# Big-head attention with scores as three float32r products of two-term splits

## The chip, the cores and the metric

The program runs on one core of a Trainium2 chip. The metric is the device time of one launch in microseconds, lower is better. The kernel before was timed three times: 2041.05, 2045.54 and 2047.98 us, median 2045.54 us. The profile shown here is one further execution, whose span from the first to the last instruction is 2040.1 us.

## The reference, cut to what matters

The reference is a two-layer transformer over 2048 tokens of width 128. Each layer is an attention followed by a mixture of experts. The change is in the attention of the second layer that has eight heads of 128:

```
qkv = einsum('bnc,fc->bnf', xn, w_qkv)            # xn: 2048 x 128, normalised
q, k, v = ...                                     # 8 heads of 128
sim  = einsum('bihd,bjhd->bhij', q * 128**-0.5, k)
sim  = where(j > i, -max, sim)                    # causal
attn = softmax(sim)
out  = einsum('bhij,bjhd->bihd', attn, v)  ->  x @ w_out
```

Everything is float32, and the scores and products are computed in float32 (the small-head attention elsewhere in the kernel uses bfloat16 terms).

## The kernel before, in words

The stage is `big_head_attention`, from about 874 to 1449 us of the span. Weights are folded beforehand: for each head, `A[:, h, :]` is the product of the query and key weights and `B` the product of the value and output weights. So a score tile is x (keys) times G, where G = A of the head times x (queries), and head outputs are added straight into `X`.

Work is cut into 32 *atoms*: a block of 512 queries and a head, (qb, h). Blocks 1 and 0 come first, alternating for each head, so the even atoms 0 to 14 are qb 1 and the odd atoms 1 to 15 are qb 0; then eight atoms of qb 2 (16 to 23), and eight of qb 3 (24 to 31). An atom has 4(qb+1) tiles of 128 keys, of which the last four lie on the diagonal and are 512, 384, 256 and 128 queries wide. Its life is:

1. `query(a)`: TensorE forms G in PSUM bank 5 (`G_BANK`, L2086), ScalarE copies it to `GT` (L2146).
2. `score(a, kt)`: TensorE forms one tile in one of five banks (L2103), ScalarE copies it to `ST` (L2158), GpSimd masks a diagonal tile (L2044), VectorE folds it into a running maximum `M` (L2204, L2207).
3. `reduce`: GpSimd takes the maximum over the partitions (L2052). Then the event `subtract`: VectorE subtracts it from all tiles of the atom (groups of four tiles L2215, the four diagonal ones L2219), and ScalarE takes the exponential (L2165, L2169).
4. `product(a, kt, half)`: TensorE multiplies by the values (L2122), in two halves of the atom; after each half VectorE divides and adds to `X` (`accumulate`, L2228 and L2232).

During the first atoms TensorE also forms the values (L2093). `ST` holds eight groups of four tiles, so for qb 2 and 3 only two atoms are under way at once: scores of atom a+1 come before the products of atom a.

The order of all this is one list, `plan.events`, laid by `KeyPlan`. Every engine walks the same list in order and takes its own part of each event, with semaphores between the engines. `KeyPlan` runs a clock of its own: each event advances it by an assumed cost. A score tile costs 0.02 + columns/600 us, a query 0.86, a product 0.265 for each 128 columns. Some events go in when that clock passes a due time: `reduce` of an atom right after the first event that follows its scores, and `subtract` 4.5 us after that, at the first event that is *not* a score (line `while self.spreads and event[0] != "score" and ...` of `emit`). Where a block normalisation for the next stage is due (events `measure`, `normalize`, `fold` behind atom 27) it is placed by that clock too.

A `query(a+1)` stands at the head of the scores of atom a, so G is formed a whole atom ahead; `GT` has three buffers, and the scores of atom a+1 are the first to need its copy.

Elsewhere, in the opening of the first stage, a table `place` of 0 and 1 is made for the small-head attention: VectorE clears it (L2374) and GpSimd fills it with 24 small copies from the identity (L2371), before it starts on its share of the first rotation.

Of the kernel before, what the change touches and what calls it, by code (L numbers as in the profile page):

```python
# [15 lines left out]
F32 = mybir.dt.float32  # L16
BF16 = mybir.dt.bfloat16
# [233 lines left out]
def small_head_stage(core, tag, src_T, w, bias, cs, arrived, KS, QS, V, place, kbias, OT, causal, order, beyond,  # L251
# [20 lines left out]
    with ExitStack() as st:  # L272
# [86 lines left out]
        with nc.Block() as block:  # L359
# [160 lines left out]
            def _(pe):  # L520
# [27 lines left out]
                def place_set(s, v):  # L548
# [9 lines left out]
                    for t in range(TERMS):  # L558
                        for i, u in enumerate(SETS[v]):
                            rows = slice(32 * i, 32 * (i + 1))  # L560
                            mm = pe.matmul(ps[:, 4 + i, :], place[rows, which, t, u, :],
# [1298 lines left out]
class KeyPlan:  # L1860
# [8 lines left out]
    def __init__(self):  # L1869
# [14 lines left out]
        self.wide0 = [sum(n - 1 for n in self.groups[:a]) for a in range(len(self.atoms) + 1)]  # L1884
        self.events = []
        self.clock, self.turns, self.spreads, self.norms = 0.0, [], [], []
        self.asked = 0
        self.lay()

# [9 lines left out]
    def emit(self, event, us):  # L1899
# [6 lines left out]
        while self.norms and self.clock >= self.norms[0][0]:  # L1906
            self.events.append(self.norms.pop(0)[1])

    def turn(self):
        _, a = self.turns.pop(0)  # L1910
        self.events.append(("reduce", a))
        if a == NORM_ATOM:
            behind = max(n for n, (qb, h) in enumerate(self.atoms) if qb in EARLY_BLOCKS)
            for n, g in enumerate(EARLY_BLOCKS):
                self.norms += [(self.clock + 0.5 + n, ("measure", g, behind)), (self.clock + 12.0 + 2 * n, ("normalize", g)),
                               (self.clock + 17.0 + 3 * n, ("fold", g))]
# [7 lines left out]
    def score(self, a):  # L1924
        if a + 1 < len(self.atoms):
            self.emit(("query", a + 1), 0.86)
        for kt in range(self.tiles[a]):
            self.emit(("score", a, kt), 0.02 + (BLK - self.first_col(a, kt)) / 600.0)
        self.turns.append((self.clock, a))

    def lay(self):
        NA = len(self.atoms)
        values = [(t, c) for t in range(NT) for c in range(2)]
        sent = 0
        self.emit(("query", 0), 0.86)
        for a in range(NA):
# [50 lines left out]
def big_head_attention(core, tag, xnT, X, raw, hpad, gamma, beta):  # L1987
# [15 lines left out]
    with ExitStack() as st:  # L2003
# [5 lines left out]
        GT = sb("GT", [P, 3, BLK])  # L2009
        M, row = sb("M", [P, 2, BLK]), sb("row", [P, 2, BLK])  # L2010
        rec = sb("rec", [P, 2, TPB])
        call = sb("call", [P, 3, 8])
# [6 lines left out]
        g_ready, g_done, s_ready, copied, masked = (sem(n) for n in ("g_ready", "g_done", "s_ready", "copied", "masked"))  # L2019
# [11 lines left out]
        with nc.Block() as block:  # L2031
# [37 lines left out]
            def _(pe):  # L2069
                asked, folded = [0], [0]  # L2070

                def fold(g):
                    pe.wait_ge(g_done, asked[0])
# [5 lines left out]
                def query(a):  # L2079
                    qb, h = plan.atoms[a]  # L2080
                    if a:
                        pe.wait_ge(g_done, a)
                    if folded[0]:
# [3 lines left out]
                              start=True, stop=True).then_inc(g_ready, 1)  # L2087

# [8 lines left out]
                def score(a, kt):  # L2097
                    n, c = plan.tile0[a] + kt, plan.first_col(a, kt)
                    if kt == 0:
                        pe.wait_ge(g_done, a + 1)  # L2100
# [27 lines left out]
                for event in plan.events:  # L2128
                    if event[0] == "query":
                        query(event[1])  # L2130
                    elif event[0] == "value":
# [9 lines left out]
            def _(act):  # L2141
                def query(a):
                    act.wait_ge(g_ready, a + 1)
# [424 lines left out]
```

## Time and profile before

| | |
|---|---|
| runs | 2041.05, 2045.54, 2047.98 us |
| span of the profiled execution | 2040.1 us |
| TensorE matmul busy | 1822.2 us (89%) |
| VectorE busy | 1547.6 us (76%) |
| ScalarE busy | 1380.9 us (68%) |
| GpSimd busy | 415.4 us (20%) |

The profiler took one execution; the program's time around that span is not in the trace. A matmul's busy time is from its start to a modelled end, so back-to-back matmuls overlap and a group of n of them lasts less than n times the mean of one: the pace of a stream is read from where a group starts and how many stand in it. "Idle before" is the time for which an engine had nothing to do before an instruction, with the instruction that ended it. A float32 matmul of the program is two MATMUL instructions in the trace, each with a weight load of its own.

### The profile page before, as it was taken

To read this page: it belongs to the slowest core of one execution; us is meant where nothing else is said; L and a number is where in the kernel's file an instruction comes from. 1 tells how busy PE (TensorE), PEld (TensorE's weight loads), DVE (VectorE), ACT (ScalarE), POOL (GpSimd) and SP (SyncE) were. 2 spreads that over 40 slices of the span, in tenths; PEclk is the share of its full clock that TensorE was granted. 3 is DMA by queue.
4 is the path that set the end of the run, shared out by engine and by line. 5 is a ranking of instruction groups with operands and counts; after the bars stand their busy time and mean duration, and the time that the engine had idled before them with its cause. 6 is when DMAs were issued, how large, how long until landed. Compare 5 with 4: busy or idle time off the path is not lost. (4 is left out here: it accounts for less than half of the span.)

```text
span 2040.1 us, 39849 instructions
## 1 busy us (share of the span) xinstructions
PE 1822.2 (89%) x15560; PEld 907.5 (44%) x15560; DVE 1547.6 (76%) x2263; ACT 1380.9 (68%) x2565; POOL 415.4 (20%) x650
## 2 busy tenths in 40 slices
PE   6699999999999798489989999999778999999784
PEld 2122222222223388435667776767512322233384
DVE  5899999999997443446767777877578979886434
ACT  3499999999999643255645656566347898888331
POOL 4201000000002324323432121221330101123413
PEclk8699999999999998889999999999867999999598
DMA  5000000000000378400000000000100000000274
GB/s 168 1 3 3 5 10 4 5 9 5 8 7 7 107 264 284 124 0 1 1 1 1 1 1 1 1 1 1 53 1 2 5 3 12 5 12 6 60 262 154
DMA packets 52874, 81.51 MB, mean 40 GB/s; under 512 B 9200, under 2 KB 37744, under 8 KB 52560
## 3 DMA queue, kind: packets, MB, share of 16 engines
q1 hardware_dynamic: 47520, 70.50, 10.9%
q0 software_dynamic: 3072, 6.30, 1.0%
q8 instruction: 124, 2.03, 0.4%
q10 hardware_dynamic: 2096, 2.17, 0.4%
q14 instruction: 62, 0.51, 0.1%
HBM read 64.13 MB, written 12.06 MB: 37 GB/s over the span
## 5 line engine op out<-in xcount | busy, mean ns | idle before, releaser
L826 DVE TENSOR_REDUCE a_mx<-psum 128x2 f32<-128x1024 f32 (+2 forms) x832 | 906.1, 1156 | 73.2 <-PE psum L601 40.2
L752 ACT ACTIVATE a_cs<-psum 128x512 f32<-128x512 f32 (+3 forms) x1664 | 857.0, 572 | 80.7 <-PE psum L619 62.4
L642 PE MATMUL psum<-a_cs,a_V 128*16 128x256 f32 (+1 forms) x6400 | 501.7, 384 | 20.9 <-ACT a_OD L732 9.7
L601 PE MATMUL psum<-a_KS,a_QS 48*128 48x512 bf16 (+3 forms) x1664 | 324.9, 381 | 32.9 <-DVE a_mx L826 29.7
L619 PE MATMUL psum<-a_QS,a_KS 51*128 51x512 bf16 (+3 forms) x1664 | 336.6, 378 | 4.9 <-ACT a_cs L752 3.1
L2122 PE MATMUL psum<-b_VW,b_ST 128*128 128x129 f32 x2176 | 252.5, 277 | 13.3 <-DVE X L2232 13.3
L2122 PEld LDWEIGHTS psum<-b_VW,b_ST 128*128 128x128 f32 x2176 | 248.5, 194 | 15.0 <-DVE X L2232 15.0
L619 PEld LDWEIGHTS psum<-a_QS,a_KS 51*128 51x128 bf16 x1664 | 87.7, 93 | 355.0 <-ACT a_cs L752 310.3
L2103 PE MATMUL psum<-b_GT,AT 128*128 128x512 f32 (+3 forms) x640 | 242.9, 534 | 1.6 <-ACT b_ST L2158 1.6
L642 PEld LDWEIGHTS psum<-a_cs,a_V 128*16 128x16 f32 x6400 | 107.1, 94 | 244.7 <-issue 120.2
L2207 DVE TENSOR_TENSOR b_M<-b_M,b_ST 128x512 f32<-128x512 f32 (+3 forms) x288 | 174.8, 607 | 43.1 <-ACT b_ST L2158 12.6
L2165 ACT ACTIVATE b_ST<-b_ST 128x2048 f32<-128x2048 f32 x48 | 91.7, 1911 | 137.5 <-DVE b_ST L2215 137.5
L2158 ACT ACTIVATE b_ST<-psum 128x512 f32<-128x512 f32 (+1 forms) x320 | 157.5, 535 | 38.2 <-PE psum L2103 37.0
L2103 PEld LDWEIGHTS psum<-b_GT,AT 128*128 128x128 f32 x640 | 122.6, 192 | 135.1 <-issue 116.1
L470 POOL CAST a_mterm<-a_mxr 128x16 bf16<-128x16 f32 x32 | 6.8, 212 | 703.1 <-DVE a_mxr L831 703.1
L2044 POOL TENSOR_SCALAR_AFFINE_SELECT b_ST<-b_ST 128x128 f32<-128x128 f32 x128 | 68.0, 555 | 368.8 <-ACT b_ST L2158 367.9
L601 PEld LDWEIGHTS psum<-a_KS,a_QS 48*128 48x128 bf16 x1664 | 83.6, 94 | 124.0 <-DVE a_mx L826 105.3
L1711 DVE TENSOR_TENSOR e_prod<-e_gate,psum 128x384 f32<-128x384 f32 (+1 forms) x72 | 43.3, 602 | 105.1 <-ACT e_gate L1669 104.5
L1613 PE MATMUL psum<-e_xT,e_W 128*128 128x128 f32 x876 | 113.5, 282 | 9.3 <-issue 7.9
L2215 DVE TENSOR_TENSOR b_ST<-b_ST,b_row 128x2048 f32<-128x2048 f32 x48 | 107.7, 2286 | 13.3 <-POOL b_row L2052 13.3
L1613 PEld LDWEIGHTS psum<-e_xT,e_W 128*128 128x128 f32 x876 | 107.6, 199 | 11.0 <-issue 7.7
L1669 ACT ACTIVATE e_gate<-psum 128x384 f32<-128x384 f32 (+1 forms) x72 | 38.0, 528 | 86.3 <-PE psum L1613 79.6
(225 smaller groups left out, 1514.5 us busy)
## 6 DMA issues: line engine op xcount, KB each, us to landing
e_W<-in_l_experts SPq DMA_DIRECT2D x45, 576.0 KB, 5.5
e_W<-in_l_experts SPq DMA_DIRECT2D x21, 768.0 KB, 5.8
yg<-e_yout SPq DMA_DIRECT2D x14, 256.0 KB, 6.0
xg<-zeros SPq DMA_DIRECT2D x2, 1472.0 KB, 9.8
a_cs<-in_rope ACTq DMA_DIRECT2D x4, 512.0 KB, 9.5
a_QS<-a_mrow SPq DMA_DIRECT2D x128, 3.0 KB
a_cs<-in_rope SPq DMA_DIRECT2D x1, 2048.0 KB, 7.8
a_num<-a_OD SPq DMA_DIRECT2D x120, 16.0 KB
```

Source lines behind the costliest of these rows:

```text
L601: mm = pe.matmul(ps[:, 2 * slot + half, 0:width], QS[rows, 2 * p + i, q_cols(qb, qt * P, P)], KS[rows, 2 * p + i, c * BLK:c * BLK + width] ...
L619: pe.matmul(ps[:, plan.bank(entry), c:BLK], KS[rows, 2 * p + i, kt * P:(kt + 1) * P], QS[rows, 2 * p + i, q_cols(qb, c, BLK - c)], start=T ...
L642: mm = pe.matmul(ps[32 * j:32 * j + 2 * HD, AV_BANK, a:b], V[:, kt, HPP * p + j, :], probs(e, a, b), start=(kt == 0 and half == 0), stop=last,
L752: act.activation(probs(HPP * s + j, c, BLK), ps[:, plan.bank(entry), c:BLK], ACT.Exp, scale=scale).then_inc(exp_done, 1)
L826: dve.tensor_reduce(mx[:, pk % 2, qt, 2 * i:2 * i + 2, c], banks, AX.X, ALU.max).then_inc(max_done, 1)
L1613: mm = pe.matmul(ps[:, 2 * side + n % 2, c * P:(c + 1) * P], weight(j, a, a + P), xT[:, j % 2, :], start=True, stop=True)
L2103: pe.matmul(ps[:, n % S_BANKS, c:BLK], xnT[:, kt * P:(kt + 1) * P], GT[:, a % 3, c:BLK], start=True, stop=True).then_inc(s_ready, 1)
L2122: mm = pe.matmul(ps[:, O_BANK + half, cols], ST[:, plan.at[a][kt // TPB], kt % TPB, i * P:(i + 1) * P], VW[:, kt, h, :], start=(kt == 0 an ...
L2158: act.activation(tile(a, kt), ps[:, n % S_BANKS, c:BLK], ACT.Copy).then_inc(copied, 1)
L2165: act.activation(group, group, ACT.Exp, scale=scale).then_inc(wide_exp, 1)
L2207: dve.tensor_tensor(M[:, a % 2, c:], M[:, a % 2, c:], tile(a, kt), ALU.max).then_inc(max_done, 1)
L2215: dve.tensor_tensor(group, group, row[:, a % 2, :].unsqueeze(1).broadcast_to([P, TPB, BLK]), ALU.subtract).then_inc(wide_sub, 1)
```

## The change

The scores of the big heads are no longer float32 products. The keys `xnT` are split once into a high part `XH` (rounded to float32r by a ScalarE copy) and a low part `XL` (VectorE, the difference); this is the new event `part`, for one block of 512 keys each. G is split too: ScalarE copies it rounded to `GH`, TensorE adds minus the identity times `GH` to the same PSUM bank (`remainder`), and ScalarE copies what is left there to `GL`. A score tile is then the sum of three float32r matmuls, XL·GH + XH·GL + XH·GH, in one bank. `GH` and `GL` have two buffers each where `GT` had three.

```
+                def remainder(a):                                  # TensorE
+                    pe.wait_ge(split, plan.copy["query", a])
+                    ...
+                    pe.matmul(ps[:, G_BANK, :], minus[:, :], GH[:, a % 2, :], start=False, stop=True,
+                              skip_group_check=True).then_inc(g_ready, 1)
                 def score(a, kt):
-                    pe.matmul(ps[:, n % S_BANKS, c:BLK], xnT[:, kt * P:(kt + 1) * P], GT[:, a % 3, c:BLK],
-                              start=True, stop=True).then_inc(s_ready, 1)
+                    pe.matmul(out, XL[:, keys], GH[:, a % 2, c:BLK], start=True, stop=False)
+                    pe.matmul(out, XH[:, keys], GL[:, a % 2, c:BLK], start=False, stop=False)
+                    pe.matmul(out, XH[:, keys], GH[:, a % 2, c:BLK], start=False, stop=True).then_inc(s_ready, 1)
...
+                def part(g):                                       # ScalarE
+                    act.activation(XH[:, mine], xnT[:, mine], ACT.Copy).then_inc(split, 1)
                 def query(a):                                      # ScalarE
-                    act.activation(GT[:, a % 3, :], ps[:, G_BANK, :], ACT.Copy).then_inc(g_done, 1)
+                    act.activation(GH[:, a % 2, :], ps[:, G_BANK, :], ACT.Copy).then_inc(split, 1)
+                def remainder(a):                                  # ScalarE
+                    act.wait_ge(g_ready, 2 * a + 2)
+                    act.activation(GL[:, a % 2, :], ps[:, G_BANK, :], ACT.Copy).then_inc(split, 1)
...
+                dve.tensor_scalar(minus[:, :], core.ident[:, :], -1.0, None, ALU.mult).then_inc(low, 1)
+                def part(g):                                       # VectorE
+                    dve.wait_ge(split, plan.copy["part", g])
+                    dve.tensor_tensor(XL[:, mine], xnT[:, mine], XH[:, mine].bitcast(F32), ALU.subtract).then_inc(low, 1)
```

The list of events changes with it. `part` 0 and 1 stand at its head, part 2 before the scores of atom 14 and part 3 before those of atom 22. `remainder(a+1)` stands after the third score tile of atom a. The planner's cost of a score tile is 0.02 + columns/800, and the block normalisations are placed a little differently:

```
     def score(self, a):
+        if a in self.parts:
+            self.emit(("part", self.parts[a]), 0.0)
         if a + 1 < len(self.atoms):
             self.emit(("query", a + 1), 0.86)
         for kt in range(self.tiles[a]):
-            self.emit(("score", a, kt), 0.02 + (BLK - self.first_col(a, kt)) / 600.0)
+            self.emit(("score", a, kt), 0.02 + (BLK - self.first_col(a, kt)) / 800.0)
+            if kt == 2 and a + 1 < len(self.atoms):
+                self.emit(("remainder", a + 1), 0.22)
...
-                self.norms += [..., (self.clock + 12.0 + 2 * n, ("normalize", g)), (self.clock + 17.0 + 3 * n, ("fold", g))]
+                self.norms += [..., (self.clock + 12.0 + 4 * n, ("normalize", g)), (self.clock + 16.0 + 4 * n, ("fold", g))]
```

So that the new tiles fit, `place` is cut from eight planes to two (128x3072 words to 128x768). GpSimd first adds the four column groups of the identity together (three additions of 128x32), and the 24 copies then move 16 elements for each partition instead of 64:

```
+        span = len(SETS) * 2 * HD
+        groups = [self.core.ident[:, i * span:(i + 1) * span] for i in range(P // span)]
+        pool.tensor_tensor(mine, groups[0], groups[1], ALU.add).then_inc(self.made, 1)
+        for i in range(2, len(groups)):
+            pool.wait_ge(self.made, i - 1)
+            pool.tensor_tensor(mine, mine, groups[i], ALU.add).then_inc(self.made, 1)
...
-                    pool.tensor_copy(rows, heads[:, :, j, :]).then_inc(self.made, 1)
+                    pool.tensor_copy(rows, self.heads[:, :, j, :]).then_inc(self.made, 1)
```

## Rows read from the trace of the kernel before

**Rows 1.** Busy time by stretch: us, each engine's busy (instructions), granted clock, DMA.

```profile
945.00:1050.00 105.00, 97.84 (x565) 73.31 (x565) 84.06 (x179) 59.71 (x120) 44.01 (x52) 1.00 0.00 1
1105.00:1205.00 100.00, 100.00 (x562) 72.59 (x562) 74.45 (x123) 57.82 (x95) 21.16 (x25) 1.00 0.00 1
```

**Rows 2.** Timeline, TensorE: start, us, what, count; 20 us, then one atom of qb 2.

```profile
20.20 0.83 PE L561 MATMUL psum<-a_terms,place 32*128 32x512 bf16 x12 [1.70 <-POOL a_terms L444]
...
1136.75 7.09 PE L2122 MATMUL psum<-b_VW,b_ST 128*128 128x129 f32 x62
...
1143.67 1.02 PE L2086 MATMUL psum<-AT,big_raw 128*128 128x512 f32 x2
...
1144.53 9.19 PE L2103 MATMUL psum<-b_GT,AT 128*128 128x512 f32 x24
```

**Rows 3.** Groups by line and shape: busy and mean, idle before.

```profile
L2103 PE MATMUL psum<-b_GT,AT 128*128 128x512 f32 x448 | 201.4, 600 | 1.6 <-ACT b_ST L2158 1.6
```

**Rows 4.** Timeline, 1137 to 1157 us (atoms 19 and 20, qb 2): VectorE, ScalarE, GpSimd.

```profile
1139.47 4.49 DVE L2215 TENSOR_TENSOR b_ST<-b_ST,b_row 128x2048 f32<-128x2048 f32 x2
...
1145.81 1.53 ACT L2169 ACTIVATE b_ST<-b_ST 128x512 f32<-128x512 f32 x4
1147.24 0.57 ACT L2146 ACTIVATE b_GT<-psum 128x512 f32<-128x512 f32 x1
...
1148.87 7.85 DVE L2207 TENSOR_TENSOR b_M<-b_M,b_ST 128x512 f32<-128x512 f32 x11
...
1156.82 1.78 POOL L2052 PARTITION_ALL_REDUCE b_row<-b_M  x1 [0.87 <-DVE b_M L2207]
```

**Rows 5.** Timeline, 1011 to 1051 us (atoms 11 and 12, qb 0 and 1; last row atom 14's end).

```profile
1015.35 1.78 POOL L2052 PARTITION_ALL_REDUCE b_row<-b_M  x1 [0.87 <-DVE b_M L2207]
...
1017.52 4.67 DVE L2207 TENSOR_TENSOR b_M<-b_M,b_ST 128x512 f32<-128x512 f32 x7
...
1022.11 2.53 DVE L2219 TENSOR_TENSOR b_ST<-b_ST,b_row 128x512 f32<-128x512 f32 x4
1022.29 2.15 POOL L2052 PARTITION_ALL_REDUCE b_row<-b_M  x1 [0.87 <-DVE b_M L2207]
...
1025.28 2.28 DVE L2215 TENSOR_TENSOR b_ST<-b_ST,b_row 128x2048 f32<-128x2048 f32 x1
...
1030.85 0.57 ACT L2146 ACTIVATE b_GT<-psum 128x512 f32<-128x512 f32 x1
...
1050.13 0.57 ACT L2146 ACTIVATE b_GT<-psum 128x512 f32<-128x512 f32 x1
```

**Rows 6.** Timeline, atoms of qb 3: one round at 1249 us, the normalisations, the last atoms.

```profile
1249.19 0.57 ACT L2146 ACTIVATE b_GT<-psum 128x512 f32<-128x512 f32 x1
...
1250.82 11.04 DVE L2207 TENSOR_TENSOR b_M<-b_M,b_ST 128x512 f32<-128x512 f32 x15
...
1318.73 6.70 DVE L2215 TENSOR_TENSOR b_ST<-b_ST,b_row 128x2048 f32<-128x2048 f32 x3
...
1409.99 1.17 ACT L2158 ACTIVATE b_ST<-psum 128x512 f32<-128x512 f32 x2
...
1434.71 13.22 PE L2122 MATMUL psum<-b_VW,b_ST 128*128 128x129 f32 x116 [0.49 <-DVE X L2232]
```

**Rows 7.** Timeline, TensorE: matmuls that follow an idle time in brackets.

```profile
930.41 1.13 PE L2093 MATMUL psum<-big_raw,AT 128*128 128x512 f32 x2 [1.99 <-ACT b_VW L2150]
...
1054.60 8.62 PE L2122 MATMUL psum<-b_VW,b_ST 128*128 128x129 f32 x52 [3.54 <-DVE X L2232]
...
1076.12 6.07 PE L2122 MATMUL psum<-b_VW,b_ST 128*128 128x129 f32 x52 [0.78 <-DVE X L2232]
```

**Rows 8.** Busy time by stretch, as in rows 1: around those idle times.

```profile
1053.00:1060.00 7.00, 5.40 (x25) 5.40 (x26) 4.01 (x14) 1.55 (x4) 1.83 (x2) 0.51 0.00 0
...
928.00:931.00 3.00, 1.01 (x3) 0.30 (x2) 1.01 (x2) 2.36 (x7) 1.31 (x4) 1.00 0.00 0
```

**Rows 9.** Timeline, GpSimd in the opening.

```profile
8.19 4.32 POOL L2371 CAST place<-ident 128x64 bf16<-128x64 f32 x24 [7.69 <-DMA ident<-in_ident]
```

More of the change, by code:

```diff
@@ L16 @@
 F32 = mybir.dt.float32
+F32R = mybir.dt.float32r
 BF16 = mybir.dt.bfloat16
@@ L1884, in __init__ @@
         self.wide0 = [sum(n - 1 for n in self.groups[:a]) for a in range(len(self.atoms) + 1)]
+        self.reach = {g: min(a for a, n in enumerate(self.groups) if n > g) for g in range(NB)}
+        self.parts = {self.reach[g] - 2: g for g in range(2, NB)}
         self.events = []
         self.clock, self.turns, self.spreads, self.norms = 0.0, [], [], []
-        self.asked = 0
+        self.asked, self.whole = 0, False
         self.lay()
+        copies = [event[0:2] for event in self.events if event[0] in ("part", "query", "remainder")]
+        self.copy = {event: n + 1 for n, event in enumerate(copies)}
+        self.part = {event[1]: n + 2 for n, event in enumerate(event for event in copies if event[0] == "part")}
     def first_col(self, a, kt):
@@ L1905, in emit @@
             self.spread()
-        while self.norms and self.clock >= self.norms[0][0]:
+        if event[0] in ("query", "remainder"):
+            self.whole = event[0] == "query"
+        while self.norms and self.clock >= self.norms[0][0] and not (self.whole and self.norms[0][1][0] == "fold"):
             self.events.append(self.norms.pop(0)[1])
@@ L1934, in lay @@
         sent = 0
+        for g in range(2):
+            self.emit(("part", g), 0.0)
         self.emit(("query", 0), 0.86)
+        self.emit(("remainder", 0), 0.22)
         for a in range(NA):
@@ L2072, in fold @@
                 def fold(g):
-                    pe.wait_ge(g_done, asked[0])
+                    pe.wait_ge(split, plan.copy["remainder", asked[0] - 1])
                     if folded[0]:
@@ L2081, in query @@
                     if a:
-                        pe.wait_ge(g_done, a)
+                        pe.wait_ge(split, plan.copy["remainder", a - 1])
                     if folded[0]:
@@ L2130, in _ @@
                         query(event[1])
+                    elif event[0] == "remainder":
+                        remainder(event[1])
                     elif event[0] == "value":
@@ L2171, in _ @@
                 for event in plan.events:
-                    if event[0] == "query":
+                    if event[0] == "part":
+                        part(event[1])
+                    elif event[0] == "query":
                         query(event[1])
+                    elif event[0] == "remainder":
+                        remainder(event[1])
                     elif event[0] == "value":
```

46 lines of the change are left out of this document (30 added, 16 removed).

## The prediction

> **What bounds the kernel now.** I read the page's shares first, then the busy time by stretch over the stage, then the timeline of one atom in each of its three regimes, and last what TensorE's clock did after idle times.
>
> The first view invites a simple answer: TensorE is 93% busy where atoms of qb 1 and 0 alternate and 100% where qb 2 runs; the others stay near 80% or below [rows 1]. A cheaper score would then come off the time whole. The timelines say otherwise, so the reader should look there for a second loop.
>
> An atom of qb 2 has 12 score tiles in 24 instructions, worth 10.5 full tiles by their columns; less the last one's drain of 0.2 they take 9.0 of their 9.19 us [rows 2], so a full tile is 0.858 us, 0.429 an instruction. There are 448 such instructions, 224 full tiles [rows 3]. A query is the same 0.86 us. Products run at 0.112 us an instruction: 62 in 7.09 with the last one's 0.26 us drain [rows 2]. So TensorE needs for an atom of qb 2: 0.86 + 9 x 0.858 + 1.31 (diagonal tiles of 384, 256 and 128 columns in proportion) + 84 x 0.112 = 19.3 us.
>
> The other loop does not contain TensorE. ScalarE copies the tiles of atom a, VectorE folds them into the maximum, GpSimd reduces, VectorE subtracts, ScalarE exponentiates, and only then, in ScalarE's order, come G's copy and the tiles of atom a+1. In atom 20 [rows 4]: G's copy starts at 1147.24, folds end at 1148.87 + 7.85 = 1156.72, the reduction ends at 1158.60. The subtraction and exponentials then take what they took one atom earlier: subtraction starts at 1139.47, exponentials end at 1147.34, when the next G copy may start. That is 11.36 + 7.87 = 19.23 us. The folds in it stand at 0.795 us a full tile (11 in 7.85, the last three narrower: 0.795 is the step of the full ones in the timeline), though one tile comes every 0.858 from TensorE: five banks were filled ahead. Hence they are VectorE's own pace, and no faster score shortens them. TensorE and this loop are within 0.1 us of each other in qb 2.
>
> In qb 3 the loop is 24.5 us: G's copy 1249.19, folds end at 1250.82 + 11.04 = 1261.86, reduction 1.9, three subtractions 6.7 and the diagonal ones 1.6, tail 1.7 [rows 6, 4]. TensorE needs 0.86 + 13 x 0.858 + 1.31 + 116 x 0.112 = 26.3. There it is the bound, with 1.8 us to give for each atom. In the pairs of qb 1 and 0 the copies of G behind an even atom's exponentials stand 19.28 us apart (1030.85 and 1050.13 [rows 5]), while TensorE's work for a pair is 2 x 0.86 + 6 x 0.858 + 2 x 1.31 + 72 x 0.112 = 17.5. VectorE's chain sets that: the even atom's folds end at 1017.52 + 4.67 = 1022.19, subtraction of the odd atom 2.53, and GpSimd's reduction of the even atom (1022.29 to 1024.44) is hidden beneath it, so the even atom's subtraction starts at 1025.28.
>
> **The change part by part.**
>
> *Score tile on TensorE.* No float32r instruction is in the trace. Bounds: a float32 instruction of the trace takes 0.429 for 512 columns, so three such would be 1.29 us a tile (dearer than 0.858 by half). A one-pass product is bf16: 12 instructions over four row groups, three rounds, in 0.83 us with a drain of 0.38 leave 0.22 us a round [rows 2], so three are 0.65. I take 0.65, the row that moves one pass: a split into terms of fewer bits is what one pass can hold. For narrow tiles I take the same rate down to a floor of 0.11 an instruction, the shortest pace with its own weight load in rows 2: 0.49, 0.33, 0.33 against 0.65, 0.43, 0.22. In all TensorE gives back 224 x 0.21 + 32 x 0.15 = 52 us, less 32 remainders at 0.22 = 7: 45 us. The page "TensorE: Matmul & The Clock Gate" of the Trainium skill (LDWEIGHTS) gives a weight load as columns over 1.2, 107 ns for 128; the trace's 0.112 agrees. Without that floor the 128-wide tile would be 0.17, and the five rounds below would each be 0.15 us shorter.
>
> *qb 2, from atom 19 on.* The loop of 19.23 stays. GL's copy (0.57) lies between third and fourth tile, where ScalarE copies every 0.48 and VectorE takes 0.795: hidden. TensorE now needs 17.4 and waits about 1.8 us at each remainder, behind G's copy. Saving: 0.
>
> *Atom 14's end to atom 19.* Here TensorE was late. Before: from 1050.13 [rows 5] to G's copy of atom 19's round at 1147.24 - 19.25 = 1128.0, 77.9 us. After: products of atoms 11 and 12 end at +11.4, query and first tile +12.9, folds of atom 16 +13.7 to +22.1, subtraction +24.1 to +30.2, exponentials +32.0, then two loops of 19.2: +70.4. Saving 7.5.
>
> *qb 3.* Seven rounds from 1224.3 to the last at 1409.5 took 185.2. After: 7 x 24.5, plus 3.4 for the three variances that fill the time before 1318.73 [rows 6] beyond the reduction, plus 5.0 for ScalarE's stores and scalings in atom 28: 179.9. Saving 5.3. From 1409.99 the last atom ran to 1447.9, 37.9 us; now its scores end at +7.3, products of atom 30 at +20.2, its own (13.0) at +33, less 0.4: saving 5.2.
>
> *Pairs of qb 1 and 0: the order.* Reading `emit` with the new list: `subtract` of an odd atom is due 4.5 us after its scores on the planner's clock, at the first event that is no score. Before, that was the first product behind the even atom's eight tiles. Now a `remainder` stands after the third tile, at 2.65 + 0.86 + 2.0 + 0.2 = 5.7 on that clock, and `subtract` goes in there: atoms 5, 7, 9, 11, 13, five rounds. ScalarE's copies of tiles 4 to 8 are thereby queued behind the odd atom's exponentials, VectorE's folds behind its subtraction, and the even atom's reduction loses its cover. With G's copy at 0: odd folds end 3.7, three even folds 5.7 to 7.9, subtraction to 9.6 (1.7 with GpSimd idle), exponentials 10.3, fourth copy 10.8, folds 10.85 to 14.05 (masks included), reduction 15.9, subtraction 19.9, exponentials 21.6. Against 19.28: +2.3 a round.
>
> *Pairs: the clock.* In such a round TensorE also stops at the remainder until G's copy, and was done 5 to 6 us before. After 3.54 us idle, the products at 1054.60 took 8.62 for 52, against 6.07 after 0.78 idle [rows 7]; the granted clock from 1053 to 1060 was 0.51, that is 1.2 instead of 2.4 GHz. After 1.99 us idle it stayed 1.00 [rows 7, 8]. With some 4.5 us at the low level, 2.2 us of work come late; the path remainder, tile, products of the odd atom, query, first even tile (4.2 us) feeds the even folds: they start at 7.9 instead of 5.7. +2.1 more, 4.4 in all. The first round has an idle time of 2.4, so I take 3.0 for it: 3.0 + 4 x 4.4 = 20.6 lost. Bounds: 5 x 2.3 = 11.5 without clock falls, 5 x 5.6 = 28 with low stretches of the 6 us seen at 1054.60. The same page of the skill says that "the default state is throttled, and activity releases the throttle"; these rows agree.
>
> *Parts.* 0 and 1 run while TensorE forms the first G. Part 2 and 3 put a copy of 0.6 us in ScalarE's loop (as the 0.57 copy of rows 4): 1.1 lost. The values' stretch (874 to 940) gains 1.5, half a microsecond for each of its three even atoms, whose folds TensorE fed one by one. *Opening.* 24 copies in 4.32 us [rows 9] are 0.18 each for 64 elements; a quarter of that plus three additions gives 3.8, so 0.5 earlier; bounds -1.2 and +0.6. The clearing of `place` is before them and nothing waits for its length.
>
> *Sum.* 20.6 + 1.1 - 7.5 - 5.3 - 5.2 - 1.5 - 0.5 = +1.7 on the 2040.1 of the profile, which is its span; the runs' median lies 5.4 higher, so 2047 us.
>
> **The rivals.**
>
> *Full gain.* TensorE stays the bound and gives back its 45 us: 2000. For it: 100% busy [rows 1]. Against: 19.23 us loops without it, at the folds' own pace. Half-way, with VectorE faster than I hold, 2025.
>
> *The order costs, the clock doesn't fall:* 11.5 in place of 20.6, so 2038. For it: 1.99 us idle left the clock alone; against: 3.54 did not, and 5 to 6 are coming.
>
> *Slower: the rounds stretch further.* One mechanism: low clock at each resumption delays the even atom's first tile, hence its folds, hence the next G copy, so idle times lengthen to 7 us. It decides from 5 us of low clock: 28 to 33 lost in the five rounds, 2055 to 2060.
>
> *Float32r isn't one pass.* At 0.429 a product (upper bound above) TensorE's gain turns into 224 x 0.43 + 20 + 14 = +130, and hardly any of it is hidden: about 2165.
>
> **How the numbers follow.** Below 0.3%, 6 us, a measurement of this kernel can't be told from no change. Chances: forecast 0.42 (2041 to 2054), no clock fall 0.20 (2034 to 2041), full or half gain 0.12, stretched rounds 0.18, not one pass 0.08. Faster by over 6 us: 0.12 and most of the second, 0.28. Slower by over 6: 0.18 + 0.08 and the upper edge of the forecast, 0.35. Within: 0.37. Range 2030 to 2064: it leaves out the not-one-pass case and the full gain. The likeliest case's own is 2041 to 2054.
>
> **What would show it.** Right: float32r instructions 0.21 to 0.22 us apart; copies of G in the even rounds of atoms 6 to 14 some 23 to 24 us apart, with 5 us of TensorE idle before each remainder and granted clock 0.5 behind it; exactly 19.2 in qb 2 with TensorE under 95% busy; 24.5 in qb 3; folds still 0.795 apart. Wrong: copies of G less than 19 apart in qb 2, which would mean that VectorE's folds follow TensorE; rounds of 19.3 in the pairs, which would mean that the order costs nothing.

## The result and the profile after

The changed kernel took 2062.05 us (median of 4 runs, 2060.96 to 2062.59); the kernel before took 2046.76 us over the 4 runs that stand beside it (2041.05 to 2051.25). The ratio is 1.0077, 95% interval 1.0058 to 1.0096: slower by 15.3 us. The range of 2030 to 2064 holds it, by 2 us at its upper edge. The predicted 2047 is 15 us too low, and the likeliest case's own 2041 to 2054 misses it by 8. One execution was slow, of the last experiment: it took 2729.96 us at a granted clock of 0.57 and is left out of the median there.

The profiled execution spans 2060.8 us against 2040.1, and its granted clock is 0.92 against 0.94. I measure "the stage" as the time from the first query matmul on the big heads to the end of the last product: 573.4 us before, 588.5 after, +15.1. All the rest of the span was 1466.6 before and 1472.3 after, but over the profiles of six variants that leave it alone it lies anywhere from 1462.2 to 1475.5. So the stage is enough to explain the medians, and nothing finer can be read from the rest.

In the changed kernel L2104 is the query, L2181 the copy of G's high part, L2111 the remainder, L2185 the copy of G's low part, L2131 to L2133 the three score products, L2197 the tile copies, L2257 the folds, L2265 and L2269 the subtraction, L2151 the products with the values, L2278 and L2282 their accumulate. First the groups by line and shape, which answer to [rows 3] (busy us, mean ns of one, idle before):

```profile
L2131 PE MATMUL psum<-b_GH,b_XL 128*128 128x512 f32 x224 | 103.0, 460 | 0.0
L2132 PE MATMUL psum<-b_GL,b_XH 128*128 128x512 f32 x224 | 89.4, 399 | 0.0
L2133 PE MATMUL psum<-b_GH,b_XH 128*128 128x512 f32 x224 | 89.3, 399 | 0.0
L2111 PE MATMUL psum<-b_GH,b_minus 128*128 128x512 f32 x32 | 16.9, 527 | 46.7 <-ACT b_GH L2181 46.7
```

The mean of one includes its drain; the starts in the timeline are 0.227 to 0.228 us apart at full clock. A full tile thus costs 0.684 us where two float32 instructions cost 0.858: the scores did become cheaper. The last row is where TensorE now stops: 46.7 us of waits at the remainders for the copy of G, where the scores before waited 1.6 in all [rows 3]. 25 of them stand before the six remainders from 955 to 1075, in the pairs.

The stretches (columns as in [rows 1]; the pairs end later now, so the first is longer):

```profile
945.00:1070.00 125.00, 104.25 (x632) 93.17 (x630) 78.17 (x174) 59.76 (x127) 37.77 (x54) 0.88 0.00 1
1001.00:1008.00 7.00, 5.05 (x24) 4.96 (x25) 2.82 (x9) 3.69 (x10) 3.25 (x5) 0.53 0.00 0
...
1110.00:1210.00 100.00, 93.24 (x637) 83.35 (x637) 76.01 (x128) 60.15 (x102) 22.16 (x25) 1.00 0.00 1
```

In the pairs the granted clock is 0.88 on average, with stretches at half speed; before it was 1.00. In qb 2 TensorE fell from 100% to 93%, and no time came of it.

One pair's round in the timeline (start, us, engine, line, what, count, idle before and its releaser), which answers to [rows 5]:

```profile
1026.16 0.57 ACT L2181 ACTIVATE b_GH<-psum 128x512 fp32r<-128x512 f32 x1
...
1026.78 0.80 PE L2111 MATMUL psum<-b_GH,b_minus 128*128 128x512 f32 x1 [4.55 <-ACT b_GH L2181]
...
1027.91 4.17 PE L2151 MATMUL psum<-b_VW,b_ST 128*128 128x129 f32 x20
...
1031.92 1.02 PE L2104 MATMUL psum<-AT,big_raw 128*128 128x512 f32 x2
...
1034.29 0.43 DVE L2254 COPY b_M<-b_ST 128x512 f32<-128x512 f32 x1 [1.36 <-ACT b_ST L2197]
...
1034.99 1.49 DVE L2257 TENSOR_TENSOR b_M<-b_M,b_ST 128x512 f32<-128x512 f32 x2 [0.27 <-ACT b_ST L2197]
...
1036.39 1.69 DVE L2269 TENSOR_TENSOR b_ST<-b_ST,b_row 128x512 f32<-128x512 f32 x4
...
1038.57 1.88 ACT L2197 ACTIVATE b_ST<-psum 128x512 f32<-128x512 f32 x5
1039.18 0.69 DVE L2257 TENSOR_TENSOR b_M<-b_M,b_ST 128x512 f32<-128x512 f32 x1 [1.09 <-ACT b_ST L2197]
...
1042.63 1.78 POOL L2070 PARTITION_ALL_REDUCE b_row<-b_M  x1 [0.88 <-DVE b_M L2257]
```

The order, the idle time and the slow products are as foretold. The odd atom's subtraction (L2269) stands between the third and the fourth fold of the even atom, ScalarE's fourth copy comes only at 1038.57, and the reduction at 1042.63 has no subtraction above it. TensorE was idle for 4.55 us before the remainder, and the 20 products behind it take 4.17 us, 0.21 each where 0.112 is the full pace. The next copy of G starts at 1050.02, 23.86 after this one.

From stage start to end, in us:

| part of the stage | before | after | gain (-) or loss | foretold |
|---|---|---|---|---|
| first query to atom 4's exponentials | 79.3 | 77.4 | -1.9 | -1.5 |
| five rounds, to atom 14's exponentials | 96.4 | 119.3 | +22.9 | +20.6 |
| to G's copy in atom 19's round | 77.9 | 74.0 | -3.9 | -7.5 |
| to G's copy of the first qb 3 round (with part 3) | 96.3 | 96.8 | +0.5 | +1.1 |
| seven rounds of qb 3 | 185.7 | 183.1 | -2.6 | -5.3 |
| first tile copy of atom 31 to last product | 37.9 | 38.0 | +0.1 | -5.2 |

Each column is one profile, and the clock moves some of these parts by itself. The first part has the same list of work in all nine profiles with float32r, where it takes 77.4 to 80.1, and in all three without, 78.7 to 82.7; it is longest where the clock was low for two stretches in it. So its -1.9 is no reading, and stages that differ by 2 or 3 us can't be told apart unless the parts show where.

### The profile page after: what moved, and what is told of

Same layout as the page of the kernel before. It is cut to its first block and busy times, and to the rows that moved or that the text cites. A ratio compares the mean times of both kernels' runs of the same rounds, so it can differ in the third digit from the quotient of the medians.

```text
span 2060.8 us, 40602 instructions
## 1 busy us (share of the span) xinstructions
PE 1816.8 (88%) x15912; PEld 979.4 (48%) x15912; DVE 1545.3 (75%) x2268; ACT 1391.5 (68%) x2601; POOL 412.6 (20%) x653
## 3 DMA queue, kind: packets, MB, share of 16 engines
q10 hardware_dynamic: 2096, 2.17, 0.4%
## 5 line engine op out<-in xcount | busy, mean ns | idle before, releaser
L602 PE MATMUL psum<-a_KS,a_QS 48*128 48x512 bf16 (+3 forms) x1664 | 330.5, 389 | 30.2 <-DVE a_mx L827 27.9
L2151 PE MATMUL psum<-b_VW,b_ST 128*128 128x129 f32 x2176 | 261.9, 284 | 5.6 <-DVE X L2282 5.6
L2151 PEld LDWEIGHTS psum<-b_VW,b_ST 128*128 128x128 f32 x2176 | 257.7, 200 | 6.2 <-DVE X L2282 6.2
L2257 DVE TENSOR_TENSOR b_M<-b_M,b_ST 128x512 f32<-128x512 f32 (+3 forms) x288 | 175.4, 609 | 44.5 <-ACT b_ST L2197 13.4
L2197 ACT ACTIVATE b_ST<-psum 128x512 f32<-128x512 f32 (+1 forms) x320 | 154.0, 538 | 10.7 <-PE psum L2133 2.9
L2131 PE MATMUL psum<-b_GH,b_XL 128*128 128x512 f32 (+1 forms) x320 | 130.6, 408 | 0.0
L2265 DVE TENSOR_TENSOR b_ST<-b_ST,b_row 128x2048 f32<-128x2048 f32 x48 | 107.8, 2287 | 19.7 <-POOL b_row L2070 19.7
L2133 PE MATMUL psum<-b_GH,b_XH 128*128 128x512 f32 (+1 forms) x320 | 118.9, 372 | 0.0
L2132 PE MATMUL psum<-b_GL,b_XH 128*128 128x512 f32 (+1 forms) x320 | 118.9, 372 | 0.0
```

Of the source, the lines that this page charges most:

```text
L602: mm = pe.matmul(ps[:, 2 * slot + half, 0:width], QS[rows, 2 * p + i, q_cols(qb, qt * P, P)], KS[rows, 2 * p + i, c * BLK:c * BLK + width] ...
L2131: pe.matmul(out, XL[:, keys], GH[:, a % 2, c:BLK], start=True, stop=False)
L2132: pe.matmul(out, XH[:, keys], GL[:, a % 2, c:BLK], start=False, stop=False)
L2133: pe.matmul(out, XH[:, keys], GH[:, a % 2, c:BLK], start=False, stop=True).then_inc(s_ready, 1)
L2151: mm = pe.matmul(ps[:, O_BANK + half, cols], ST[:, plan.at[a][kt // TPB], kt % TPB, i * P:(i + 1) * P], VW[:, kt, h, :], start=(kt == 0 an ...
L2197: act.activation(tile(a, kt), ps[:, n % S_BANKS, c:BLK], ACT.Copy).then_inc(copied, 1)
```

## The experiments

Six kernels take the loss apart, four test the loop of qb 2. "Round" is the distance between the exponentials' ends of atoms 4, 6, 8, 10, 12 and 14.

**The order alone.** The kernel before, with the odd atoms' subtraction moved to where the change puts it:

```
 (in score(), behind the third tile)
+            while kt == 2 and self.spreads and self.clock >= self.spreads[0][0]:
+                self.spread()
```

> The float32 kernel of before, with one difference: the subtraction of an odd atom (5, 7, 9, 11, 13) goes in behind the third score tile of the even atom, where the changed kernel has it. Scores, buffers and planner costs stay. Theory (the order alone uncovers the even atom's reduction and queues five tile copies behind the odd exponentials): the copies of G that end a round stand 21.4 to 21.8 us apart for five rounds instead of 19.3, so the qb 2 atoms begin 10 to 12 us later; TensorE goes ahead with its products as before, so its idle times stay under 3 us and the clock stays up. Some is given back where TensorE was late behind atom 15; total 2052 to 2058. Rival (the order costs nothing, all of the loss is TensorE stopped at the remainder and its clock): rounds of 19.3 and 2046.

2054.44 against 2042.99 us, ratio 1.0055 (1.0032 to 1.0077). The timeline of ScalarE:

```profile
1022.92 0.57 ACT L2148 ACTIVATE b_GT<-psum 128x512 f32<-128x512 f32 x1
...
1043.91 0.57 ACT L2148 ACTIVATE b_GT<-psum 128x512 f32<-128x512 f32 x1
```

The rounds are 21.0, five times: +1.7 each, 8.5 in all. The stage is 5.5 longer (578.9), because other parts came out shorter: 0.6 in the first part and 1.6 in qb 3, where the list of work is the same and the clock wasn't low behind a TensorE idle time of 2.5 us, and 0.9 before atom 19, where TensorE was late anyway. The order costs time without any float32r in the kernel. It isn't the clock either: this was low from 981 to 984 and from 1022 to 1025, in some of the rounds and not in others, and all five are 20.99. My +2.3 was too much, and 21.0 lies below the 21.4 to 21.8 expected. The medians lie 11 us apart, of which the stage of this profile shows half.

**The order put back.** The changed kernel, whose remainder no longer lets the subtraction in:

```
-        while self.spreads and event[0] != "score" and self.clock >= self.spreads[0][0]:
+        while self.spreads and event[0] not in ("score", "remainder") and self.clock >= self.spreads[0][0]:
```

> The changed kernel with the subtraction of odd atoms back behind the even atom's eight tiles (a remainder no longer counts as a place for it). Theory: the uncovered reduction and the queued copies go, about 2.3 us of the 4.6 lost in each of five rounds; TensorE still stops at the remainder until G's copy and so still falls to the low clock where the idle time stays over 3 us, so rounds of 20.0 (no fall) to 22 us instead of 23.9, total 2046 to 2053. Rival (all of the loss is the remainder's stop and the clock): rounds stay near 24 and 2061.

2047.28 us, ratio to before 1.002 (1.0004 to 1.0035): 13 us of the stage are back (575.5), 14.0 in the rounds and 1.6 at the end, less 2.0 behind the pairs and 0.7 in the first part. The timeline of ScalarE and TensorE:

```profile
982.12 0.57 ACT L2181 ACTIVATE b_GH<-psum 128x512 fp32r<-128x512 f32 x1
...
1004.13 0.57 ACT L2181 ACTIVATE b_GH<-psum 128x512 fp32r<-128x512 f32 x1
1024.55 0.57 ACT L2181 ACTIVATE b_GH<-psum 128x512 fp32r<-128x512 f32 x1
1025.17 0.50 PE L2111 MATMUL psum<-b_GH,b_minus 128*128 128x512 f32 x1 [3.34 <-ACT b_GH L2181]
```

Rounds of 22.1 and 22.0 where the granted clock fell (962 to 966, 983 to 986 us) and of 20.4 where it stayed up: the same work behind idle times of 3.33 and 3.34 us, 1.6 us apart by the clock alone. That leaves 1.1 us a round over the 19.3 of before, for the stop at the remainder.

**The stop taken away too.** The same kernel, with the odd atom's remainder behind its products, where G's copy is long done:

```
+    def late(self, a):
+        return self.atoms[a][0] == 0 and a >= 5
 ...
+        if a and self.late(a - 1):
+            self.emit(("remainder", a), 0.22)
 ...
-            if kt == 2 and a + 1 < len(self.atoms):
+            if kt == 2 and a + 1 < len(self.atoms) and not self.late(a):
```

> As the kernel with the subtraction behind the tiles, and the remainder that follows an odd atom's scores (from atom 5 on) goes behind that atom's products, just ahead of the next query, so TensorE no longer stops before its products. Theory: both costs are gone, VectorE's chain alone sets the pairs, 19.3 to 19.8 us a round, qb 2 stays at 19.25 and qb 3 at 24.6; total 2036 to 2042, that is 0.2 to 0.5% under the kernel before. Rival (a further cost of float32r in the pairs, such as ScalarE's extra copy): rounds over 20.5 and no gain over the kernel before.

2041.27 us, ratio 0.9996 (0.9978 to 1.0013). Rounds of 19.5, 19.5, 19.5, 19.5, 19.9; stage 569.2, which is 4.2 less than before. The pairs' loss is gone (1.5 us of 22.9 are left), and it was more than the whole loss. What float32r brings on this kernel shows only here: 4 us of the stage, 2.6 of them in the seven rounds of qb 3, which take 182.7 to 183.2 in all six profiles with whole folds and the remainder of qb 3 behind the third tile, against 185.7. In the medians it is no more than can be told from no change.

**The clock kept up.** The changed kernel, with five float32 products of 512 columns into a free score bank, issued ahead of the remainders in the pairs:

```
+                    if a in (6, 8, 10, 12, 14, 16):
+                        n = plan.tile0[a - 1] + 3
+                        pe.wait_ge(copied, n - S_BANKS + 1)
+                        for _ in range(5):
+                            pe.matmul(ps[:, n % S_BANKS, :], A[:, 0, :], xnT[:, 0:BLK], start=True, stop=True)
```

> The changed kernel, and while TensorE would wait for G's copy before the remainders of atoms 6, 8, 10, 12, 14 and 16 it runs five float32 products of 512 columns (4.3 us) into a free score bank that the next tile overwrites. Nothing is computed from them. Theory (the low clock behind each idle time delays the even atom's first tile): the granted clock stays at 1.00 from 960 to 1080, rounds shrink from 23.9 to 21.8 us, total 2052 to 2056. Rival (the low clock hits only work that has time to spare): rounds stay at 23.9 and 2061.

2051.75 us, ratio 1.0051 (1.0036 to 1.0066); stage 581.3, 7.2 less than the changed kernel. A stretch and a part of the timeline:

```profile
960.00:1066.00 106.00, 104.55 (x616) 83.23 (x615) 70.81 (x159) 55.88 (x120) 34.66 (x50) 1.00 0.00 1
```

```profile
1026.41 0.57 ACT L2186 ACTIVATE b_GH<-psum 128x512 fp32r<-128x512 f32 x1
1027.03 0.50 PE L2116 MATMUL psum<-b_GH,b_minus 128*128 128x512 f32 x1 [0.27 <-ACT b_GH L2186]
...
1048.07 0.58 ACT L2186 ACTIVATE b_GH<-psum 128x512 fp32r<-128x512 f32 x1
```

The granted clock is 1.00 throughout. The last three rounds are 21.7 instead of 23.9, though TensorE does more work and its remainders wait for the same copies. So the low clock costs 2.2 us in such a round. The first two are 23.5 and 22.0, against 23.3 and 24.5: in the first the added products end 1.6 us after G's copy and hold the remainder up themselves. With the order put back and the clock up it was 20.4, so the moved subtraction costs 1.3 on top of the stop; the stop itself is 0.9 (20.4 against 19.5). These shares hold in this order of taking them off: the subtraction moved alone cost 1.7, and the clock with the order put back 1.6.

**The last atom.** The changed kernel, with the first half of atom 30's accumulate placed between the group subtractions of atom 31:

```
 (VectorE, in the loop over the group subtractions)
+                        if a == NA - 1 and g == 1:
+                            accumulate(a - 1, 0)
 (and where it stood)
-                        accumulate(event[1], event[3])
+                        if (event[1], event[3]) != (NA - 2, 0):
+                            accumulate(event[1], event[3])
```

In the trace of the changed kernel these rows of the timeline (VectorE, TensorE) are why:

```profile
1441.86 6.70 DVE L2265 TENSOR_TENSOR b_ST<-b_ST,b_row 128x2048 f32<-128x2048 f32 x3 [1.92 <-POOL b_row L2070]
1448.47 1.70 DVE L2269 TENSOR_TENSOR b_ST<-b_ST,b_row 128x512 f32<-128x512 f32 x4
1450.09 0.16 DVE L2278 RECIPROCAL b_rec<-psum 128x2 f32<-128x2 f32 x1
...
1450.95 14.86 PE L2151 MATMUL psum<-b_VW,b_ST 128*128 128x129 f32 x116 [2.64 <-DVE X L2282]
```

Atom 31's products may not overwrite their bank before the accumulate of atom 30 has read it, and that is queued on VectorE behind all of atom 31's subtraction. TensorE is idle for 2.64 us and then runs at half clock from 1451 to 1455: 14.86 us for what takes 13.17 at full clock.

> The changed kernel, and VectorE adds the first half of atom 30 to X behind two of the three group subtractions of atom 31, instead of behind all of its subtraction. Theory (the last products wait for the accumulator bank, whose reading stands behind that subtraction, and the idle time of 2.6 us brings the low clock): products of atom 31 start about 2.5 us earlier, right behind those of atom 30, the clock stays at 1.00 there, and the stage ends 2 to 4 us earlier against the round before it; total too near 2061 to tell. Rival (the exponentials hold the last products): the end stays 38.0 us behind the first tile copy of atom 31.

2050.61 us, ratio 1.0043 (1.0028 to 1.0058). The timeline of both engines now:

```profile
1433.30 26.12 PE L2151 MATMUL psum<-b_VW,b_ST 128*128 128x129 f32 x232
...
1444.41 0.16 DVE L2280 RECIPROCAL b_rec<-psum 128x2 f32<-128x2 f32 x1
```

The products of atoms 30 and 31 run in one piece, 232 in 26.12 us. From the first tile copy of atom 31 to the end it is 33.5 us instead of 38.0: -4.5 in the trace, and the stage is 584.0. By the ratios, 1.0077 and 1.0043, it is 7 us, but their intervals touch; I take the trace's 4.5. Not all of that is the wait. The kernel with the order put back has the same list of work at its end, the same wait, and a clock that stayed at 1.00 (TensorE):

```profile
1444.41 13.22 PE L2151 MATMUL psum<-b_VW,b_ST 128*128 128x129 f32 x116 [2.64 <-DVE X L2282]
```

There it is 36.4 us to the end, and in the kernel with the late remainder as well. So moving the accumulate is worth 2.9, and the other 1.6 was the clock, which fell behind this wait in two profiles of four.

**Both repairs.** The late remainder and the last atom's edit together:

> The kernel with the subtraction behind the tiles and the late remainder for odd atoms, and the early reading of atom 30's first half. Theory: rounds of 19.5, 19.25 and 24.6 us as measured without the last edit, and 2 to 4 us off the end: the stage takes 565 to 567 us against 573.4 before, and the total is 5 to 9 us under the kernel before, a ratio of 0.996 to 0.998. Rival (the end is not on the path of what follows): no change against the kernel without the edit, 2041.

2038.19 us (12 runs) against 2045.2, ratio 0.997 (0.9954 to 0.9986); stage 565.9. This version beats both kernels, the one before by 0.3%.

**Narrow folds, before and after.** The folds of full tiles in qb 2 and 3 take 16 columns instead of 512, so VectorE's part of the loop all but vanishes (most of the maximum is then left out):

```
+                        top = BLK if qb < 2 or kt >= TPB * qb else 16
-                        dve.tensor_tensor(M[:, a % 2, c:], M[:, a % 2, c:], tile(a, kt), ALU.max)
+                        dve.tensor_tensor(M[:, a % 2, c:top], M[:, a % 2, c:top], tile(a, kt)[:, 0:top - c], ALU.max)
```

> The kernel of before with VectorE's maximum of the full, undiagonal tiles behind the first taken over 16 columns instead of 512, in atoms of qb 2 and 3 (the rest of those columns is left out of the maximum). That takes about 0.5 us off each of 7 (qb 2) or 11 (qb 3) folds and so opens the loop without TensorE to 15.6 and 19. Theory (two loops of equal length in qb 2, TensorE's the longer in qb 3): TensorE holds both, rounds stay at 19.3 and 26.3 and the stage loses under 5 us. Rival (VectorE alone bound them): rounds of 16 to 17 in qb 2.

The kernel before: 2043.78 against 2045.2 us, ratio 0.9984 (0.9964 to 1.0004), rounds in qb 2 still 19.26, TensorE 100% busy from 1110 to 1210, and the seven rounds of qb 3 at 185.7 as before. There TensorE is a full bound beside VectorE.

> The changed kernel with the same narrow folds (the same part of the maximum left out). TensorE's own work for an atom of qb 2, with float32r products 0.228 us apart, 0.4 us for the first one behind a float32 product, remainder and query, is 18.3 us; of qb 3 24.6. Theory (VectorE's folds were what hid the cheaper scores in qb 2): rounds shrink from 19.25 to 18.3 to 18.8 in qb 2; they stay at 24.6 in qb 3, where TensorE's work and the other loop are equally long. Rival (the remainder's wait for G's copy holds the rounds): they stay at 19.25 or above.

The changed kernel: 2054.59 us, ratio 1.0046 (1.0023 to 1.0069), and the rounds stayed at 19.24 to 19.29 (19.8 with part 3). That was a miss. Timeline of qb 2 (ScalarE, TensorE, VectorE, GpSimd):

```profile
1167.00 0.57 ACT L2181 ACTIVATE b_GH<-psum 128x512 fp32r<-128x512 f32 x1
1167.62 0.51 PE L2111 MATMUL psum<-b_GH,b_minus 128*128 128x512 f32 x1 [1.08 <-ACT b_GH L2181]
1173.28 9.60 PE L2151 MATMUL psum<-b_VW,b_ST 128*128 128x129 f32 x84
1175.90 1.78 POOL L2070 PARTITION_ALL_REDUCE b_row<-b_M  x1 [0.87 <-DVE b_M L2258]
1177.78 0.17 DVE L2280 RECIPROCAL b_rec<-psum 128x2 f32<-128x2 f32 x1 [1.98 <-PE psum L2151]
1177.98 0.61 DVE L2284 SCALAR_TENSOR_TENSOR X<-psum,b_rec,X 128x128 f32<-128x128 f32 x2
1178.51 4.49 DVE L2267 TENSOR_TENSOR b_ST<-b_ST,b_row 128x2048 f32<-128x2048 f32 x2
```

The reduction is done at 1177.68, yet the subtraction starts at 1178.51, behind an accumulate that waited 1.98 us for products. These had started late, since tiles 4 to 12 and they stand behind the remainder, and the remainder behind the copy of G. So there is a third loop, G's copy, remainder, nine tiles, half the products, accumulate, subtraction, exponentials, and it too is 19.3 us long. I gave it no place in the prediction. In qb 3 the seven rounds went from 183.0 to 179.3, so there the folds did hold some of the time.

**The remainder at the tail.** The same, and the remainder of qb 2 and 3 behind the last score tile, which opens that third loop:

```
+    def slot(self, a):
+        return self.tiles[a] - 1 if self.atoms[a][0] >= 2 else 2
-            if kt == 2 and a + 1 < len(self.atoms):
+            if kt == self.slot(a) and a + 1 < len(self.atoms):
```

> The changed kernel with narrow folds (the maximum of full, undiagonal tiles of qb 2 and 3 over 16 columns, the rest left out), and in qb 2 and 3 the remainder stands behind the atom's last score tile instead of its third. With narrow folds alone the rounds of qb 2 stayed at 19.3: the subtraction began 0.8 us behind the reduction's end, behind the accumulate of the atom before, whose products stood behind the tiles that the remainder held back. Theory (two loops, VectorE's folds and the one through the remainder, are each 19.3): with both opened TensorE's own 18.3 us hold, rounds of 18.3 to 18.8 in qb 2. Rival (a third cause holds the round): 19.3 again.

2048.99 us, ratio 1.0021 (1.0006 to 1.0035). Timeline of ScalarE and TensorE:

```profile
1145.52 0.58 ACT L2184 ACTIVATE b_GH<-psum 128x512 fp32r<-128x512 f32 x1
...
1146.63 0.50 PE L2134 MATMUL psum<-b_GH,b_XL 128*128 128x512 f32 x1 [0.23 <-ACT b_ST L2200]
...
1163.89 0.57 ACT L2184 ACTIVATE b_GH<-psum 128x512 fp32r<-128x512 f32 x1
1182.28 0.58 ACT L2184 ACTIVATE b_GH<-psum 128x512 fp32r<-128x512 f32 x1
```

Rounds of 18.4 (18.9 with part 3), and TensorE 97.78% busy from 1110 to 1210: with both loops opened the cheaper scores come through, 0.9 us an atom. TensorE's own need, added up from its starts, is 17.9; the other 0.5 is a wait for a score bank that ScalarE hasn't copied, once an atom, as at 1146.63. So the 18.3 expected for TensorE was nearly met, but not by TensorE's work. It takes both edits: narrow folds alone left 19.24 or more, and the other alone follows.

> The version with the subtraction behind the tiles, the late remainder for odd atoms and the early reading of atom 30, and in qb 2 and 3 the remainder behind the atom's last tile. Folds are whole. Theory (VectorE's folds are a loop of their own of 19.2 us): rounds stay at 19.2 to 19.3 in qb 2 although TensorE is no longer held, 24.6 in qb 3, stage 563 to 567 us, no change of the total beyond 2 us against the version without this edit. Rival (only the remainder held qb 2): rounds of 18.3, stage 5 to 9 us shorter.

The tail remainder with full folds, on top of both repairs: 2039.41 (median of 9) against 2045.33 us, ratio 0.9981 (0.9967 to 0.9995). Rounds of 19.18 in qb 2, part 3's apart: that is VectorE's loop by itself, with no remainder in it. The stage was 568.5, a little over the 563 to 567 expected and not better than the 565.9 without the edit. The seven rounds of qb 3 are 3.2 us longer, nearly all in the one with the block normalisation's stores, 33.7 instead of 30.5. TensorE stood idle for 3.95 us in it, before a transposition, and its clock was low in 1344 to 1350, neither of which the other profile shows. Whether the tail remainder or the clock made that was not tried.

## Why the prediction was right or wrong

**Right: the mechanism of the pairs.** Foretold were copies of G 23 to 24 us apart, TensorE idle some 5 us before each remainder and a granted clock of 0.5 behind it. The rounds were 23.3, 24.5, 23.8, 23.9 and 23.9, the idle times 4.55 to 4.91 (2.17 in the first) and the clock 0.53 over 1001 to 1008. The two costs were named, and their sum was near: +22.9 instead of +20.6. The split differs from mine. I had 2.3 for the order and 2.1 for the clock in each round; the experiments give, for a late round of 23.9 against 19.3, 2.2 for the clock, 1.3 for the moved subtraction, 0.9 for the stop at the remainder with the clock up, and 0.2 that stay with the remainder moved away. That the sum of the two came within 2.3 us of 22.9 is in part luck, for the order was taken too dear and the stop was no term of its own.

**Right: qb 2 gives nothing.** Timeline of the changed kernel (ScalarE, VectorE, GpSimd), which answers to [rows 4]:

```profile
1167.13 0.57 ACT L2181 ACTIVATE b_GH<-psum 128x512 fp32r<-128x512 f32 x1
...
1168.76 7.85 DVE L2257 TENSOR_TENSOR b_M<-b_M,b_ST 128x512 f32<-128x512 f32 x11
...
1176.71 1.78 POOL L2070 PARTITION_ALL_REDUCE b_row<-b_M  x1 [0.87 <-DVE b_M L2257]
1177.91 0.17 DVE L2278 RECIPROCAL b_rec<-psum 128x2 f32<-128x2 f32 x1 [1.30 <-PE psum L2151]
...
1178.64 4.49 DVE L2265 TENSOR_TENSOR b_ST<-b_ST,b_row 128x2048 f32<-128x2048 f32 x2
...
1186.42 0.57 ACT L2181 ACTIVATE b_GH<-psum 128x512 fp32r<-128x512 f32 x1
```

Eleven folds take 7.85 us as before, and the copies of G are 19.25 to 19.29 apart, 19.76 with part 3. The reason was right but not whole: the accumulate of the third loop ends at 1178.64, within 0.2 us of the reduction's end, so two loops hold the round at 19.3 now. TensorE's "waits about 1.8 us at each remainder" was 1.08.

**Wrong in size: the three gains of TensorE.** I took 7.5 + 5.3 + 5.2 = 18.0 us off behind the pairs, and 6.4 came (3.9, 2.6 and -0.1). The failed steps are "Atom 14's end to atom 19", "qb 3" and the last atom's "saving 5.2". The first and the last have one fault: I followed scores, folds and exponentials, but not the accumulate, which holds TensorE's bank and stands in VectorE's order. Behind the pairs "two loops of 19.2" took 21.2 and 20.4, which is 3.1 of the 3.6 missing. The first goes like this (VectorE, TensorE, ScalarE):

```profile
1110.73 5.46 DVE L2257 TENSOR_TENSOR b_M<-b_M,b_ST 128x512 f32<-128x512 f32 x8 [0.47 <-ACT b_ST L2197]
1116.11 0.16 DVE L2278 RECIPROCAL b_rec<-psum 128x2 f32<-128x2 f32 x1
...
1116.97 9.65 PE L2151 MATMUL psum<-b_VW,b_ST 128*128 128x129 f32 x84 [1.94 <-DVE X L2282]
...
1127.52 0.60 ACT L2181 ACTIVATE b_GH<-psum 128x512 fp32r<-128x512 f32 x1 [1.53 <-PE psum L2104]
```

Atom 16's products are ready to start at 1115.0 and wait 1.94 us for atom 15's accumulate, queued behind the folds of atom 17. The next query stands behind those products, and G's copy then waits 1.53 us for it. In the second loop the subtraction stands behind an accumulate that waited 1.77 us for its products. With narrow folds and the tail remainder the first wait was 0.76 and the first loop 19.2, the second still 20.4. The gain of 3.9 itself owes something to the long rounds ahead of it: with the late remainder, behind short rounds, this stretch takes 75.6 to 76.8 in three profiles, a gain of 1.1 to 2.3.

In the last atom it is the same wait, and [rows 6] showed it already in the profile before, as 0.49 us with "<-DVE X" as its releaser. An earlier TensorE made it 2.64, and the clock fell on top. That this was the last atom's loss is shown by moving the accumulate: 4.5 of the 5.2 us came, 2.9 from the wait and 1.6 from the clock. Behind the pairs the accumulate was not moved, so there its part is argued from the timeline and not shown.

In qb 3 TensorE's own work for an atom is 0.86 + 0.23 + 13 x 0.684 + 1.16 for the diagonal tiles + 116 x 0.112 = 24.1 us by the paces after, where those of the prediction give 23.7: a full tile was taken at 0.65 and takes 0.684. That still lies under the loop of 24.5, so the pace isn't what failed. Most of the 2.7 us missing stand in two rounds: 25.3 for the one behind the first remainder of qb 3, where TensorE had stood idle for 3.76 us and its clock was low from 1270.4 to 1273.8, and 30.9 for the one with the stores, where 29.5 was foretold and TensorE stood idle for 3.50 us before the remainder, with a low clock behind it. The others were 24.65 to 24.92 where no store or variance was in the way. The prediction had these stops and the clock at nothing in qb 3. What they cost was not tested, and in other profiles of the same work the two rounds were 26.3 and 29.8 with the same sum; the cause of this part stays open.

**The sum.** +1.7 was foretold and +15.1 came in the stage. The 13.4 between are 3.6 + 2.7 + 5.3 for the three gains, 2.3 for the pairs, 0.5 for the opening's gain, which lies outside the stage and can't be told from its changes, less 0.4 for the values' stretch and 0.6 for the parts.

**The rivals.** The full gain is ruled out by 19.3 us rounds, the dearer float32r by a pace of 0.228, the steady clock by 0.53. "Stretched rounds" (2055 to 2060) was nearest in time, but right for another reason: its mechanism would have made the idle times grow to 7 us and the rounds to 25, and they were 4.55 to 4.91 and, but for one of 24.5, under 24. "The clock doesn't fall" leaned on 1.99 us idle having left it alone [rows 7]; the same profile has 1.99 us before the value products at 901.10, and there the clock was low from 902.9 to 906.3.

## What to carry to other kernels

Before counting a gain on the busiest engine, list every loop that returns to the same point with its length: here VectorE's (19.18 to 19.23) and the one through the remainder (19.28) lay within 0.1 us of each other and of what TensorE had needed before, and only opening both let a 20% cheaper score tile through. A bank that is read by an engine further down the chain is such a loop; a short "<-DVE X" idle time before is what becomes the long one after. When a list of work is written out by a planner, look first at which event the new one will let in: one small matmul moved a subtraction and a stop into five rounds, cost 21 us of them, and was repaired with a few lines.

## What the runs showed of the hardware

- A float32r product of 128 x 128 x 512 runs at 0.228 us, where I had taken 0.65 a tile, 0.217 a product; 384 columns take 0.171 to 0.178, 256 take 0.117 to 0.127. At 128 columns the second and third product of a tile take 0.112, but the first only 0.058 (1112.31 to 1112.37). The Trainium skill's page "TensorE: Matmul & The Clock Gate" (LDWEIGHTS) gives a weight load as columns over 1.2, 107 ns for 128 columns; the trace's 0.112 agrees. The 0.058 says nothing against it: the weight load of that first product is recorded from 1112.19, beneath the 256 columns of the product before it.
- A float32r product behind a float32 one costs nothing extra, though its own recorded time looks like it:

```profile
1126.46 1.02 PE L2104 MATMUL psum<-AT,big_raw 128*128 128x512 f32 x2
1126.92 0.80 PE L2131 MATMUL psum<-b_GH,b_XL 128*128 128x512 f32 x1
1127.55 0.40 PE L2132 MATMUL psum<-b_GL,b_XH 128*128 128x512 f32 x1
```

  The second instruction of the query starts at 1126.89 and takes 0.43, but the float32r product behind it has a start 0.03 later. From the query's start to the tile's second product it is 1.09 us, which is 0.86 + 0.23. The 0.4 us "for the first one behind a float32 product" in the expectation of the narrow folds is this misreading; without it TensorE needs 17.9 us for an atom of qb 2 and 24.1 for one of qb 3.
- Of the same length of idle time the clock made different things. In the kernel with the order put back 3.33 us before the remainder at 982.74 were followed by half speed from 983 to 986, and 3.34 us before the one at 1004.76 left it at 1.00. Five products without use in such a gap kept it up in all rounds, and the stage was 7.2 us shorter.
